# Compressed attention values: low parts of the probabilities on the other half of the partitions

## What is computed

```python
q = rmsnorm(apply_partial_rope(q, cos, sin), q_norm_w)          # 2 x 16 heads x 1024 tokens x 128
ck = rmsnorm(h.reshape(b, nb, M * HID) @ W_comp, k_norm_w)      # one key per 16 tokens: nb = 64
valid = blk_end[None, :] < pos[:, None]
c_scores = jnp.einsum('bhtd,bnd->bhtn', q, ck) * scale
c_out = attend(c_scores, valid[None, None], sink, ck, 'bhtn,bnd->bhtd')
...
sw_out = attend(sw_scores, sw_mask[None, None], sink, v_sw, 'bhts,bsd->bhtd')
ao = (c_out + sw_out)...
```

## Time and profile before

| | us |
|---|---|
| median of 3 runs (1076.89 to 1080.45) | 1079.01 |
| the profiled execution | 1077.91 |
| its span, first to last instruction | 1076.0 |
| PE busy, share of the span | 971.9 (90%) |
| PEld | 821.5 (76%) |
| DVE | 650.0 (60%) |
| POOL | 554.5 (52%) |
| ACT | 540.2 (50%) |
| products of the compressed values, busy (384 of 128x256) | 54.8 |

### The profile page before, as it was taken

One profiled execution on the slowest core, in us unless ns is written; L12 is line 12 of the kernel. 1 busy time (PEld: TensorE's weight loads), 2 busy tenths in 40 slices (PEclk: granted clock), 3 DMA queues, 4 the chain that ended last, 5 costly groups with the idle time before them and its releaser, 6 DMA issues.

```text
span 1076.0 us, 16635 instructions
## 1 busy us (share of the span) xinstructions
PE 971.9 (90%) x5062; PEld 821.5 (76%) x5062; DVE 650.0 (60%) x1202; ACT 540.2 (50%) x1493; POOL 554.5 (52%) x758
## 2 busy tenths in 40 slices
PE   5787879669999999999999999999748999999996
PEld 5677758458888888888888888888536777878784
DVE  1764354547777777777877777777459543242312
ACT  1563342247677776776767777676222322414221
POOL 0263000068888888877888888887203222221221
PEclk9997888869999999999999999999959999999999
DMA  7547741231313213122141231410090010020101
GB/s 237 174 158 260 295 146 59 79 105 32 124 45 106 69 50 128 45 101 71 39 139 31 89 98 39 139 33 6 21 398 2 1 43 37 1 79 1 40 0 41
DMA packets 52572, 95.68 MB, mean 89 GB/s; under 512 B 9905, under 2 KB 27057, under 8 KB 49713
## 3 DMA queue, kind: packets, MB, share of 16 engines
q1 hardware_dynamic: 41904, 66.61, 19.1%
q10 hardware_dynamic: 10624, 28.52, 7.4%
HBM read 77.42 MB, written 26.35 MB: 96 GB/s over the span
## 4 chain that ended last, share of the span: by engine, by line
PE 59%; issue 10%; DVE 5%; POOL 3%; ACT 2%; DMA 1%; POOLq 0%; ACTq 0%; DVEq 0%; SPq 0%
PE banks L921 41%; PE banks L1421 7%; PE banks L1386 4%; POOL gus L1563 3%; PE banks L960 3%; PE banks L937 2%; PE banks L969 1%; DVE arena L1514 1%; DVE z L1512 1%; DVE stats L1485 1%; DVE qn L1137 1%; DVE prob L1152 1%; DVE ws L1154 1%; DMA arena<-x_mid 1%; ACT prob L1062 0%
## 5 line engine op out<-in xcount | busy, mean ns | idle before, releaser
L921 PE MATMUL banks<-fold,aoT 128*128 128x512 f32 x768 | 201.9, 400 | 2.0 <-DVE aoT L1093 2.0
L1421 PE MATMUL banks<-hT,w_hi 128*128 128x512 f32 x704 | 176.1, 402 | 3.2 <-DVE hT L1500 2.0
L1421 PEld LDWEIGHTS banks<-hT,w_hi 128*128 128x128 f32 x704 | 133.0, 191 | 36.4 <-DVE hT L1500 3.6
L1563 POOL TENSOR_TENSOR gus<-arena,gus 128x512 fp32r<-128x512 f32 x44 | 59.6, 1355 | 191.8 <-ACT gus L1464 191.8
L921 PEld LDWEIGHTS banks<-fold,aoT 128*128 128x128 f32 x768 | 136.8, 188 | 24.6 <-DVE aoT L1093 2.5
L921 PE MATMUL banks<-k_st,qT 128*128 128x320 f32 x768 | 131.3, 321 | 0.0
L921 PEld LDWEIGHTS banks<-k_st,qT 128*128 128x128 f32 x768 | 116.2, 193 | 0.2
L1533 DVE SCALAR_TENSOR_TENSOR arena<-banks,sg,arena 128x512 f32<-128x512 f32 x44 | 33.0, 749 | 126.2 <-ACT arena L1459 126.2
L921 PE MATMUL banks<-pp,v_st 128*128 128x512 f32 x384 | 104.5, 407 | 0.0
L1386 PE MATMUL banks<-w_hi,gus 128*128 128x512 f32 x352 | 91.9, 403 | 10.2 <-POOL gus L1563 8.0
L1459 ACT ACTIVATE arena<-banks,sg 128x512 f32<-128x512 f32 x44 | 30.3, 689 | 140.9 <-PE banks L1421 140.9
(11 more groups left out here) (175 smaller groups left out, 1997.9 us busy)
## 6 DMA issues: line engine op xcount, KB each, us to landing
arena<-in_wq_blocks ACTq DMA_DIRECT2D x8, 1056.0 KB, 4.9
wq_words<-in_wq_blocks ACTq DMA_DIRECT2D x8, 1056.0 KB, 6.9
w_lo<-wq_words SPq DMA_DIRECT2D x11, 768.0 KB, 15.0
go_raw<-in_w_go SPq DMA_DIRECT2D x16, 512.0 KB, 7.3
arena<-in_L_attn_h SPq DMA_DIRECT2D x16, 256.0 KB, 8.1
comp_raw<-in_w_comp SPq DMA_DIRECT2D x16, 256.0 KB, 5.0
v_parts<-v_out ACTq DMA_DIRECT2D x4, 1024.0 KB, 4.6
k_st<-k_parts SPq DMA_DIRECT2D x32, 128.0 KB, 2.7
```

The source lines that it names most:

```text
L921: last = pe.matmul(out, lhs[a], rhs[b], start=start and q == 0 and u == 0, stop=stop and q == n - 1 and u == 2)
L1421: last = pe.matmul(GU[2 * (n % 2) + w][:], parts[a][:, h, cols], hT[:, c % 2, x, k], start=(k == 0 and q == 0), stop=(k == KC - 1 and q == ...
L1563: pool.tensor_tensor(gus[:, n % 2, 1], gu[:, n % 2], gus[:, n % 2, 0].bitcast(F32), ALU.subtract).then_inc(gu_lo, 1)
```

## The change

The table of values loses its padding: `ck_pad` holds, on both halves of the partitions, the same 64 rows of `ck`, in a high and a low part. The transposed probabilities are laid out anew in `pcS[partition, slot, pair, half, token]`. For a head of half 0, the high part stays on partitions 0 to 63, where T has it, and the low part is written to the same columns of partitions 64 to 127; for half 1 the high part is on 64 to 127 and the low part on 0 to 63. One product with the high values then sums both over its 128 partitions: v_hi·(p_hi + p_lo). A second with the low values adds v_lo·(p_hi + p_lo), which includes v_lo·p_lo, a term that was left out before. So `compressed_values` is two products of 512 columns, whose output is the whole of O.

In return the high and the low part are written by two instructions each, one for each half of the partitions, 64 partitions by 256 columns; VectorE's write to partitions that they don't read from. In the front, the four pieces of `ck_pad` become one instruction of 128x256 on ScalarE and one on VectorE, its memset goes, and the table's store and loads halve.

```diff
@@ -95,7 +95,7 @@
         q_parts = dram("q_parts", [TILES, P, 2, P])
         k_parts = dram("k_parts", [BATCH * (TPB + 1), P, 2, P])
         v_parts = dram("v_parts", [TILES, P, 4, P])
-        ck_parts = dram("ck_parts", [BATCH, P, 4, P])
+        ck_parts = dram("ck_parts", [BATCH, P, 2, P])
         ckq_parts = dram("ckq_parts", [BATCH, P, 2, NB])
         wq_words = dram("wq_words", [P, HB * WB])
         x_tok = x_in.rearrange("b t c -> (b t) c")
@@ -174,7 +174,7 @@
         ccol=([P, KC, BATCH], F32), modT=([P, 2 * KC, BATCH], F32), stats=([P, CHUNK, 6], F32),
         meanvar=([P, CHUNK, 2], F32), rstd=([P, CHUNK, 1], F32), minus_half=([P, CHUNK], F32), kss=([P, CHUNK], F32),
         kr=([P, CHUNK], F32), kw_col=([P, 1], F32), qw_col=([P, 1], F32), kqw=([P, 1], F32), kw_row=([P, D], F32), ck_raw=([P, P], F32), ck_sq=([P, P], F32),
-        ck_nd=([P, D], F32), ck_dup=([P, BATCH, 2, NB], F32), cs1=([P, 2], F32), ck_pad=([P, BATCH, 2, 2, P], F32R), ckT=([P, BATCH * NB], F32),
+        ck_nd=([P, D], F32), ck_dup=([P, BATCH, 2, NB], F32), cs1=([P, 2], F32), ck_pad=([P, BATCH, 2, P], F32R), ckT=([P, BATCH * NB], F32),
         ckq=([P, BATCH, 2, NB], F32R))
     return {name: sb(scope, name, shape, dt) for name, (shape, dt) in spec.items()}
 
...
@@ -420,17 +420,14 @@
                 last = act.activation(ck_dup[:, b, half], ckT[:, b * NB:(b + 1) * NB], ACT.Copy)
         last.then_inc(ck_act, 1)
         act.wait_ge(ck_pe, 3)
-        for b in range(BATCH):
-            for half in range(2):
-                rows = slice(half * NB, (half + 1) * NB)
-                last = act.activation(ck_pad[rows, b, half, 0], bank[3][rows, b * P:(b + 1) * P], ACT.Copy)
-        last.then_inc(ck_act, 1)
+        act.activation(ck_pad[:, :, 0], bank[3][:, 0:BATCH * P].rearrange("p (b n) -> p b n", b=BATCH), ACT.Copy
+                       ).then_inc(ck_act, 1)
 
         for n in range(4, STEPS):
             go_high(n)
             if n == 4:
                 act.wait_ge(ck_dve, 3)
-                act.dma_start(ck_parts.rearrange("b p a n -> p b a n"), ck_pad[:].rearrange("p b h a n -> p b (h a) n").bitcast(F32)
+                act.dma_start(ck_parts.rearrange("b p a n -> p b a n"), ck_pad[:].bitcast(F32)
                               ).then_inc(zero_stored, 16)
                 act.wait_ge(ckq_lo, 1)
                 act.dma_start(ckq_parts.rearrange("b p a n -> p b a n"), ckq[:].bitcast(F32)).then_inc(zero_stored, 16)
...
@@ -552,12 +548,8 @@
         dve.scalar_tensor_tensor(ckq[:, :, 1], bank[2][:, 0:P].rearrange("p (b n) -> p b n", b=BATCH), qw_col[:, 0:1],
                                  ckq[:, :, 0].bitcast(F32), ALU.mult, ALU.subtract).then_inc(ckq_lo, 1)
         dve.wait_ge(ck_act, 5)
-        for b in range(BATCH):
-            for half in range(2):
-                rows = slice(half * NB, (half + 1) * NB)
-                last = dve.tensor_tensor(ck_pad[rows, b, half, 1], bank[3][rows, b * P:(b + 1) * P],
-                                         ck_pad[rows, b, half, 0].bitcast(F32), ALU.subtract)
-        last.then_inc(ck_dve, 1)
+        dve.tensor_tensor(ck_pad[:, :, 1], bank[3][:, 0:BATCH * P].rearrange("p (b n) -> p b n", b=BATCH),
+                          ck_pad[:, :, 0].bitcast(F32), ALU.subtract).then_inc(ck_dve, 1)
 
         for n in range(4, STEPS):
             go_low(n)
...
@@ -814,7 +806,7 @@
     rope_st = sb(scope, "rope_st", [P, 2, P])
     k_st = sb(scope, "k_st", [P, 2, 2, KEYS], F32R)
     v_st = sb(scope, "v_st", [P, 2, 2, 2, P], F32R)
-    ck_st = sb(scope, "ck_st", [P, 2, 2, 2, P], F32R)
+    ck_st = sb(scope, "ck_st", [P, 2, 2, P], F32R)
     sq = sb(scope, "sq", [P, HG, D])
     ss = sb(scope, "ss", [P, 2, HG])
     rq = sb(scope, "rq", [P, 2, HG])
@@ -834,7 +826,7 @@
     csm = sb(scope, "csm", [P, 2, HG])
     crs = sb(scope, "crs", [P, 2, HG])
     pc = sb(scope, "pc", [P, 2, HG * NB])
-    pcT = sb(scope, "pcT", [P, 2, 2, 2 * P], F32R)
+    pcS = sb(scope, "pcS", [P, 2, 2, 2, P], F32R)
     aoT = sb(scope, "aoT", [P, 2, 2, WG], F32R)
     x_t = sb(scope, "x_t", [P, 2, C])
     y_t = sb(scope, "y_t", [P, C])
@@ -984,12 +976,9 @@
 
             wait(pe, "cT_lo", g.n())
             wait(pe, f"c_in{g.tile_slot}", g.loaded())
-            cp = ck_st[:, g.tile_slot]
-            out = O[:].rearrange("p (pair half n) -> p half pair n", half=2, n=P)
-            for half in range(2):
-                last = three(out[:, half], [((cp[:, half, 0], cp[:, half, 1]),
-                                             tuple(pcT[:, g.slot, part].rearrange("p (pair n) -> p pair n", n=P)
-                                                   for part in range(2)))], start=False, stop=half == 1)
+            for part in range(2):
+                last = pe.matmul(O[:], ck_st[:, g.tile_slot, part], pcS[:, g.slot].rearrange("p a h n -> p (a h n)"),
+                                 start=False, stop=part == 1)
             last.then_inc(s["cv_mm"], 1)
 
         def project(g, heads):
@@ -1033,7 +1022,10 @@
         def compressed_high(g):
             wait(act, "cT_mm", g.n())
             wait(act, "cv_mm", g.n(2))
-            act.activation(pcT[:, g.slot, 0], T[:, 0:2 * P], ACT.Copy).then_inc(s["cT_hi"], 1)
+            for half in range(2):
+                rows = slice(half * NB, (half + 1) * NB)
+                last = act.activation(pcS[rows, g.slot, :, half], T[rows, 0:2 * P].rearrange("p (a n) -> p a n", n=P), ACT.Copy)
+            last.then_inc(s["cT_hi"], 1)
 
         def squares(g):
             wait(act, "q_mm", g.n())
@@ -1118,8 +1110,11 @@
 
         def compressed_low(g):
             wait(dve, "cT_hi", g.n())
-            dve.tensor_tensor(pcT[:, g.slot, 1], T[:, 0:2 * P], pcT[:, g.slot, 0].bitcast(F32),
-                              ALU.subtract).then_inc(s["cT_lo"], 1)
+            for half in range(2):
+                rows, across = slice(half * NB, (half + 1) * NB), slice((1 - half) * NB, (2 - half) * NB)
+                last = dve.tensor_tensor(pcS[across, g.slot, :, half], T[rows, 0:2 * P].rearrange("p (a n) -> p a n", n=P),
+                                         pcS[rows, g.slot, :, half].bitcast(F32), ALU.subtract)
+            last.then_inc(s["cT_lo"], 1)
 
         def masked_low(g):
             wait(dve, "p_lo", g.n())
@@ -1271,7 +1266,7 @@
             free("cv_mm", GPT * (t - 1))
             sp.dma_start(v_st[:, slot].rearrange("p a b n -> p (a b) n").bitcast(F32),
                          v_parts[bass.ds(t, 1)].rearrange("t p a n -> (t p) a n")).then_inc(s[f"v_in{slot}"], 16)
-            sp.dma_start(ck_st[:, slot].rearrange("p a b n -> p (a b) n").bitcast(F32),
+            sp.dma_start(ck_st[:, slot].bitcast(F32),
                          ck_parts[bass.ds(t // TPB, 1)].rearrange("t p a n -> (t p) a n")).then_inc(s[f"c_in{slot}"], 16)
 
         def store(t, slot, nth):
```

7 lines of the change are left out of this document (3 added, 4 removed).

## The result

The changed kernel takes 1100.78 us (median of 4 runs), the one before 1078.16 on the same chip. One of the four runs took 1159.12 us at a mean granted clock of 0.82, where the others had 0.95; the ratio goes by the other three, whose median is 1099.67: 1.0199, 95% interval 1.0167 to 1.0231, so 2.0% slower. The profiled execution took 1099.67 us, its span 1097.8, which is 21.8 us more than the 1076.0 of before.

A forecast was written before the change was run, and what follows sets the result against it. TensorE's instruction stream was taken to bound attention. 56 ordinary groups x 0.41 = 23.0, 8 masked x 0.52 = 4.2, front -0.9: +26.3 on 1077.9 gives 1104.2 us; range 1098 to 1110, with rivals two and three 1089 to 1111.

The forecast's parts named there:

- The products' gain: Compressed values on TensorE: six products of 256 columns take 0.70 us, two of 512 take 0.48; gain 0.22 a group.
- The price of a half: ScalarE and VectorE: each half costs what the whole did, 0.39 and 0.42 us, without overlap; starts 0.40 and 0.44 apart.
- rivals two and three: Two: ScalarE's halves overlap, 1095.4 us, chance 0.12. Three: both engines' halves overlap, 1089.8 us, chance 0.08.
- rival four: VectorE's low parts: writing to the other half of the partitions costs extra, at most 0.54 us a group, 1139; chance 0.04.
- The load of the next transposes: TensorE's weight load for the next query's transposes, waiting for VectorE's second half: 0.76 us late, at 610.86 instead of 610.10.
- What lateness of a load costs: Transposes on TensorE: a load that waited isn't hidden, 0.10 us more for the restart; transposes come 0.63 us late.
- An ordinary group: Attention, 56 groups: transposes 0.63 us late, less 0.22 saved by the products, so 0.41 us slower each.
- A masked group: Attention, 8 groups that mask their probabilities: the loop through ScalarE's L1058 becomes 0.52 us later, TensorE's saving lies outside it.
- The front: Before attention: ck_pad's four pieces become one instruction on each engine, so TensorE's wait for go ends 0.9 us earlier.
- TensorE's busy time: Attention stage, a sign: busy time falls by 64 x 0.22 = 14 us or so while the stage grows.
- The next to be late: Ordinary groups: VectorE's qn comes 0.52 us later, the query's load on TensorE moves 0.41; 0.30 us remain.
- rival one: The saving is delivered: half the partitions cost half the time, the loop doesn't grow; 13.2 us gained, 1064.7; chance 0.08.

The follow-up runs named there:

- products_only: The changed kernel, with rounded and low part each written by one whole instruction (low parts in the wrong place); 1063.56 us, ratio 0.9875 to before.
- halves_only: The kernel before, with rounded and low part each written in two halves of the partitions, in place; 1117.09 us, ratio 1.036.
- high_halves: The kernel before, with only ScalarE's rounded part in two halves of the partitions; 1090.73 us, ratio 1.0118.
- low_halves: The kernel before, with only VectorE's low part in two halves of the partitions; 1091.40 us, ratio 1.0121.
- staggered: The changed kernel, with ScalarE signalling after each half and VectorE starting with the first; 1090.68 us, ratio 1.0127 to before.

## Why the prediction was right, point by point

The time: 1104.2 us was forecast, within 1089 to 1111, and 1100.78 came (1099.67 in the profiled run). The mechanism was the forecast's, and it was shown by undoing it from both sides (products_only, halves_only). The terms:

- **What bounds the stage.** Right. The saving of products_only reaches the end of the kernel in ordinary groups in full, and not in masked ones.
- **The products' gain.** 0.22 us a group forecast, 0.24 measured. The two products of 512 take 0.46, a little under the 0.48 taken from the spacing of the window's six.
- **The price of a half.** 0.39 and 0.42 forecast, 0.378 and 0.422 measured; the spacing 0.40 and 0.44 forecast, 0.39 and 0.43 measured. The rows of ck_pad were the right model, and rivals two and three (overlap), which had 0.20 of the chance, fall. Crossing the partitions is free (rival four falls).
- **The load of the next transposes.** 0.76 us late forecast, 0.76 measured (1.73 against 0.97 from ScalarE's start). The halves were a little shorter and the release to this load 0.07 us instead of 0.05, which cancels; with 0.07 the loop had 0.06 us to spare and not 0.08.
- **What lateness of a load costs.** 0.63 us forecast, 0.59 to 0.61 measured: from the compressed transposes to the window's values 624.73 - 622.17 = 2.56 us, before 1.97 (608.72, not among the rows, to 610.69). The restart after a wait costs some 0.06 for four transposes, not the 0.10 of the query's three products: 0.41 us from the waited load to the window's values (624.32 to 624.73), 0.36 from fed transposes to them (610.33 to 610.69), the rest rounding.
- **An ordinary group.** 0.41 forecast, 0.36 measured, the sum of those two small misses. 56 groups: 20 us instead of 23.0.
- **A masked group.** 0.52 forecast, 0.49 measured. The engine is ScalarE, as high_halves and low_halves show. That the number is this close is partly luck: a shorter mask and a later qn, neither in the forecast, nearly cancel.
- **The front.** 0.9 us forecast, 1.85 in the changed kernel's trace, 0.8 to 1.9 over all kernels with one piece. For this trace the step was mis-sized: I moved wup along with the pieces of ck_pad, and overlooked that the stores' issues, 1.35 us of nothing on ScalarE before (its copy of go done at 135.47, wup at 136.82, the latter not among the rows), would then run beside the go copy.
- **The sum over the trace.** The products' first start is 2.7 us earlier (236.6 against 239.3), the stretch to their last start 23.6 us longer (553.6 against 530.0), the rest 0.9 longer: 21.8 in all. The forecast had 27.2 for the stretch, 0.9 for the front and nothing for the rest; its stretch was 3.6 too long and its front 1.8 too small, which both made it too slow, and the rest took 0.9 off that again.
- **TensorE's busy time.** A fall of 14 us or so was named as a sign, and it fell by 3.8. The products' 64 x 0.24 = 15.4 us are there, but a product ahead of a wait counts as busy to its end, while in a stream the next starts long before that. halves_only shows this by itself: with the six products of before, an ordinary group is busy for 8.61 us of its 9.02, where it was busy for all of its 8.41 (from the trace's records). The sign was a poor one, since waits hide a saving in it.
- **The next to be late.** The prediction put the query's qn 0.30 us from being the bound. In the changed kernel 0.10 were left (qn ends at 626.30, the load starts at 626.45, and a release takes 0.05): the load now starts 0.22 us ahead of its products (626.45 to 626.67) instead of 0.11, so it moved back less than they did. It wasn't the bound yet, and staggered found it as soon as the other loop shrank.
- **Where rival one turns.** The prediction has the change break even at a growth of 0.20 us. It left out there the lead of the weight load, 0.23 us, that its own main sum counts: 0.08 + 0.23 - 0.10 + 0.22 = 0.43. high_halves bears this out, where a growth of 0.39 cost 0.18, less than the products' 0.24. The rival's time doesn't depend on it.

## What to carry to other kernels

Before splitting an instruction that only reads out a shared bank, count the loop that the bank closes: which engine may write next, what covers it, and how much is spare (here 0.08 us of slack stood against 0.84 us of growth), with half the partitions priced at the full time and no overlap between alternating halves. A saving on the bounding engine together with more cover for the loop (one head ahead of the transposes, three behind) turned the same change from 2.0% slower to 1.0% faster (0.4% of it the cover gives without the change), and each loop that was relieved after that showed the next one within 0.4 us: VectorE's queue, then the query's scale, then GpSimd's.
